# Layer 0 of a graph network: TensorE makes the counts of two steps in a row, then two steps' share of the sums

## The reference, cut to what matters

```python
h = relu(layernorm(x))                        # x: 6250 nodes x 128
def sage(h, Wl, bl, Wr):                      # 206250 edges (src, dst), sorted by dst
    msg = segment_sum(h[src], dst, 6250)
    cnt = segment_sum(ones, dst, 6250)
    return (msg / max(cnt, 1)) @ Wl.T + bl + h @ Wr.T
h = relu(batchnorm(sage(h, Wl0, bl0, Wr0)))   # layer 0: 128 -> 256
h = relu(batchnorm(sage(h, Wl1, bl1, Wr1)))   # layer 1: 256 -> 256
out = x + log_softmax(sage(h, Wl2, bl2, Wr2)) # layer 2: 256 -> 128
```

## Time and profile before

| | |
|---|---|
| median of 3 runs | 1443.36 us (1443.16 to 1446.37) |
| the profiled execution | 1447.48 us, of which the span of the core's instructions is 1445.6 us |
| layer 0 | up to about 556 us of the span |
| TensorE | busy 1347.1 us, 93% of the span |
| VectorE, ScalarE, GpSimd | busy 40%, 36% and 39% of the span |
| VectorE and ScalarE in layer 0 (60 to 545 us) | 369.66 and 385.70 of 485 us |
| granted TensorE clock | 0.997 of full speed in the mean |

### The profile page before, as it was taken

The page is one execution under the profiler, slowest core; times in us unless marked ns, Lnnn a source line. Parts: engine busy times, 40 slices in busy tenths (PEclk is TensorE's granted clock), DMA queues, the critical chain, the costliest instruction groups (busy, mean ns, idle before and its releaser), DMA issues.

```text
span 1445.6 us, 31363 instructions
## 1 busy us (share of the span) xinstructions
PE 1347.1 (93%) x13653; PEld 828.9 (57%) x13653; DVE 581.0 (40%) x1081; ACT 520.4 (36%) x848; POOL 562.7 (39%) x562
## 2 busy tenths in 40 slices
PE   1399999999998999999999999999999999899997
PEld 0277777777776778664444444444447754444445
DVE  6977767686869862221111111102102212222223
ACT  4897878778787783430000000000000520000001
POOL 3423140404132100005566666665661026566650
PEclk9999999999999999999999999999999999999999
DMA  6334554445454443446666666665652688898983
GB/s 165 99 140 165 199 197 179 169 140 209 187 205 175 144 157 99 172 137 234 203 223 218 230 226 217 227 228 181 226 180 75 199 297 297 290 322 314 327 304 99
DMA packets 91988, 291.14 MB, mean 201 GB/s; under 512 B 17539, under 2 KB 53013, under 8 KB 88613
## 3 DMA queue, kind: packets, MB, share of 16 engines
q1 hardware_dynamic: 63596, 228.73, 44.3%
q0 software_dynamic: 21824, 55.44, 12.6%
q10 hardware_dynamic: 6424, 4.88, 1.1%
HBM read 197.78 MB, written 91.22 MB: 200 GB/s over the span
## 4 chain that ended last, share of the span: by engine, by line
PE 78%; ACT 6%; DMA 5%; issue 4%; DVE 4%; POOL 3%; ACTq 0%; DVEq 0%; SPq 0%; POOLq 0%
PE bank L1603 27%; PE bank L1180 16%; PE cells L1603 12%; PE cells L1172 6%; DMA hots<-table,src_i 3%; PE bank L1856 3%; PE cells L1213 2%; POOL hots L514 2%; PE cells L1669 2%; ACT ring L650 2%; PE bank L1606 2%; ACT junk L598 2%; PE bank L1186 1%; PE bank L1188 1%; DMA parts<-in_pairs_dram,last_i 1%
## 5 line engine op out<-in xcount | busy, mean ns | idle before, releaser
L514 POOL DMA_INDIRECT hots<-table,src_i x444 | 420.5, 947 | 455.4 <-DMA table<-parts 216.8
L1603 PE MATMUL bank<-ring,parts 128*128 128x500 f16 x2058 | 463.0, 375 | 0.0
L650 ACT CAST ring<-cells 128x980 f16<-128x980 f32 (+1 forms) x325 | 337.6, 1056 | 103.0 <-PE cells L1172 96.5
L1603 PEld LDWEIGHTS bank<-ring,parts 128*128 128x128 f16 x2058 | 192.7, 96 | 226.0 <-issue 13.5
L1180 PE MATMUL bank<-ring,parts 128*128 128x250 f16 (+1 forms) x2450 | 317.8, 272 | 2.2 <-ACT ring L650 2.2
L875 DVE TENSOR_TENSOR hots<-iotas,tab 128x980 f16<-128x980 f16 (+3 forms) x262 | 245.5, 997 | 4.6 <-ACT tab L614 4.6
L1180 PEld LDWEIGHTS bank<-ring,parts 128*128 128x128 f16 (+1 forms) x2450 | 215.8, 98 | 33.8 <-ACT ring L650 3.0
L1603 PE MATMUL cells<-ring,parts 128*128 128x500 f16 (+1 forms) x980 | 215.9, 373 | 0.0
L721 ACT ACTIVATE agmg<-cells,isp 128x124 f32<-128x124 f32 x20 | 7.3, 364 | 472.9 <-PE cells L1222 472.9
L1603 PEld LDWEIGHTS cells<-ring,parts 128*128 128x128 f16 (+1 forms) x980 | 90.9, 96 | 112.7 <-issue 9.0
L1172 PE MATMUL cells<-hots 64*128 64x49 f16 x4670 | 105.6, 186 | 40.3 <-DVE hots L875 36.8
(11 more groups left out here) (211 smaller groups left out, 965.1 us busy)
## 6 DMA issues: line engine op xcount, KB each, us to landing
ring<-c_blocks SPq DMA_DIRECT2D x120, 750.0 KB, 6.1
c_blocks<-ring SPq DMA_DIRECT2D x25, 3062.5 KB, 10.7
ring<-c_blocks SPq DMA_DIRECT2D x40, 812.5 KB, 5.0
rcb<-rc_row SPq DMA_DIRECT2D x69, 125.0 KB, 8.7
hots<-table,src_i POOLq DMA_INDIRECT x444
Z<-in_x_dram SPq DMA_DIRECT2D x4, 768.0 KB, 6.4
table<-parts SPq DMA_DIRECT2D x2, 1536.0 KB
table<-parts ACTq DMA_DIRECT2D x2, 1536.0 KB
```

Of the source, the lines that this page charges most:

```text
L514: pool.indirect_dma_start(out=got[layer][:, 5 * (r % NGOT) + i, :], out_offset=None, in_=tables[layer], in_offset=bass.IndirectOffsetOnAxi ...
L650: act.copy(blk[c % 2][:, :, :].rearrange("p a (d g) -> p a d g", d=GD)[:, :, :, GPS * i:GPS * i + n], cells[t % 2][:, :, 0:n * NA].rearran ...
L1603: ins = pe.matmul(bank[b][:, 0:2 * BD].rearrange("p (s d) -> p s d", s=2), lhs, ring[0:r, :, BD * a:BD * a + BD], start=(a, part) == (0, 0 ...
```

## The change

```diff
@@ pe_layer0, in step i of round c, behind the counts
                     if c >= 1:
-                        if i == 0:
+                        if i == 1:
                             pe.wait_ge(a_cells, NST * c)
                             if c >= 3:
                                 pe.wait_ge(v_mean, c - 2)
-                        upto = len(work) * (i + 1) // NST
+
+                        upto = len(work) * (i + 1) // NST if i % 2 or i == NST - 1 else done
                         for a, part in work[done:upto]:
```

## The result

The changed kernel takes **1459.49 us** (median of 4 runs, 1457.58 to 1461.34) beside 1443.26 us of the kernel before (4 runs): a ratio of 1.0112, 95% interval 1.0093 to 1.0132. That is 16 us slower, where 1442 was forecast. The profiled execution took 1459.71 us, its span is 1457.9 us. Layer 0 ends, by the first matmul that follows it, at 570.1 us instead of 556.2; what comes after lasts as long as before (887.8 us against 889.4). So all of the loss, 13.9 us in these two executions, lies in layer 0 (they are 12.2 us apart; the medians are 16.2 apart).

What follows compares the result with a forecast made beforehand. Layer 0 was taken as bound by TensorE's list: 97 saved passage pairs at 0.21 give 20 us, nearly all given back in waits, chiefly for ScalarE's copies, leaving about 1 us: 1442 us, range 1433 to 1450.

Steps and rivals of the forecast that it cites:

- what a passage costs: TensorE's switch between counts and sums: 0.10 to 0.11 us; a joined pair takes 2.35 instead of 2.56, 0.21 less.
- The 0.80 before the counts of step 9: Steps 6 to 9: ScalarE's two L694 delay the copy of step 7, so these counts wait 0.80 us, in 18 rounds.
- the 0.08 of an ordinary pair: Joined pairs: odd counts come at 2.62 us, their buffer is free at 2.70, a wait of 0.08 for ScalarE's copy.
- the `pe_ends` rounds: Five rounds where L1158 comes 0.96 us earlier; the wait for VectorE covers the one of 0.80; gain 0.96.
- The turns' waits: Steps 10 and 11, rounds 4, 8, 12, 16, 20: waits of 0.9 or 0.4 us; loss 0.24, or 0.87 in 16 and 20.
- Steps 4 and 5: The product of 1.79 us lies between the groups, the number of passages stays, ScalarE catches up: gain 0.
- the five cycles: Gains and losses summed over cycles of four rounds: -0.02 to 0.4 up to round 13, about -0.2 each later; together +0.3.
- the samplings: Five times, over steps 11, 12, 0, 1: copies 1.90 us apart; gain of 0.11 to 0.18 kept.
- rival 3: VectorE sets the pace, covering waits for ScalarE: less than 3 us either way, 1440 to 1445; within the forecast's 0.7 chance.
- the wait in step 4 of rounds 8, 12, 16 and 20: TensorE arrives earlier than VectorE's one-hots and waits up to 0.7 us, giving back what it gained since `pe_ends`.
- Rival 1: ScalarE's copies keep up and step 9 does not wait: 18 x 0.80 come back, 1428 us; chance 0.1.
- Rival 2: TensorE and ScalarE in lockstep: copies free 0.06 us later cost 115 pairs 7 us, 1449; pair above 2.45; chance 0.2.

Runs made afterwards that it cites:

- after_spread2: The changed kernel with each block's store cut into seven pieces, issued at steps 0, 1, 2, 4, 5, 6 and 8 of the next round: 1444.1 us.
- before_spread2: The kernel before with its block store cut into seven pieces, issued at steps 0, 1, 2, 4, 5, 6 and 8 of the next round: 1445.4 us.
- before_long: The kernel before with each block stored twice, to two places, by one transfer of 6 MB: 1488.8 us, ratio 1.0295.

## Why the prediction was wrong

**Right: what a passage costs.** 2.35 us for a joined pair was forecast and 2.35 is in the trace. Steps 0 to 3 take 5.14 us before and 4.80 after in an ordinary round, a gain of 0.34, as forecast.

**Right: the waits for the copies.** The 0.80 before the counts of step 9 is 0.79; the 0.08 of an ordinary pair is the 0.1 inside the row of 0.80. About 25 us of waits were forecast. The view adds up to 19.1, in 31 pieces, and it shows 28 of them, those directly behind other counts, 0.17 too short: some 24. The wait before step 9 was forecast as 18 x 0.80 = 14.4; in after_spread2 it stands in sixteen rounds, and the delays add up to 11.9. As forecast, there is none in the `pe_ends` rounds; rounds 20 and 21 have none either.

**Right: ends and turns.** In round 3 the counts follow L1158 after 2.66 us, as forecast, and the wait shrinks to 0.64, from 1.40 in the same round before and in the earlier trace rows. The turns' waits rise from 1.2 to 3.1 us.

**So the sum holds where nothing else waits.** With the store cut and the issue waits gone the measured ratio to the kernel before is 1.0007 [0.9993, 1.0022], which takes in the forecast 0.9993. Beside its own control, before_spread2, the changed kernel is 1.35 us faster in the medians. There is some luck in how close this is. Steps 4 and 5 were put at 0 and cost 0.09 in nearly every round (4.26 us before, 4.35 after), nearly 2 us in all; the waits before step 9 were put 2.5 us too high. And the five cycles were summed as +0.3, while the terms as printed (with 0.11 for the samplings) give 0.38 - 0.02 - 0.02 - 0.23 - 0.23 = -0.1. All of this is inside the error that the prediction named. VectorE's pace, rival 3, moved no more than was allowed for it: TensorE's waits for it are 18.3 us before, 14.9 in the changed kernel and 17.5 in after_spread2, and the wait in step 4 of rounds 8, 12, 16 and 20, put at up to 0.7, shows as 0.32 at most.

**Wrong: the step that took TensorE's list for granted.** The part on what bounds the kernel says "layer 0 is bound by how fast TensorE gets through its list", and the sum was made of passages and of waits for other engines. That TensorE must also be given its instructions, 16 KB at a time, over the same DMA engines that carry 3 MB at the start of every round, has no term in it; the store itself was left out. The kernel before just manages (0.9 us in 24 rounds). The changed one runs steps 0 to 3 faster, beside the store, and runs dry: 12.9 us of issue waits, and about 1.4 us more for the half clock after the longest (0.77 + 0.32 + 0.35 for the three rows behind it). The 12.0 by which the issue waits grew and the 1.4 are 13.4 of the 13.9 us; taking the cause away gave back 15.4 us of the median. The row "issue 0.9" stood in the view that the earlier trace rows were taken from, and I left it out as small. It was the one sign in that view that this supply had little to spare.

A page had it the other way. The Trainium skill, Runtime: NRT & Kernel Launch, Instruction fetch mechanics, says that a sequencer fetches its program in blocks of 16 KiB while it runs the one before, and that crossing a block is "mostly hidden". The trace agrees on the size (111 packets, 1.82 MB) and, for the changed kernel, not on the cost: 12.9 us in layer 0.

**Rival 1 did not come true** in the changed kernel, since step 9 waits there. Its price was half right: if step 9 did not wait, 14 us were to come back, and with L694 at step 5 and no issue waits it was 7.0 us (1444.1 to 1437.0). Of the 11.9 us of delays before step 9 in after_spread2 the move takes away 9.3, and leaves the small ones of ordinary pairs and those of rounds 22 to 24; 1.3 us of it are lost again in step 11 of round 15, where a wait of 1.25 for VectorE follows. **Rival 2**, lockstep, gave the right side for the wrong reason: a pair takes 2.35 and not 2.45.

The range, 1433 to 1450, was made of errors of the terms that were there. A term that was missing is in no such range.

## What to carry to other kernels

Where an engine gets through thousands of short instructions, read the "issue" row of its waits and the DMA queue of kind "instruction" beside the large transfers: an engine that is made faster next to a transfer of megabytes may run out of program, and here one small issue wait before the change was the warning. A store that nobody awaits is then not free; two pieces with a gap of a few microseconds between them cured it here, two pieces without a gap did not, and seven pieces of which the last was issued too late cost more than the issue waits. To tell such a wait from others, look for the fetch whose end stands just ahead of it. And of two engines in turns, look for what stands between the paired copies: moving one small activation by a step was worth 7 us in the joined order and nothing in the old one.

## What the runs showed of the hardware

- A store of 3062.5 KB in one transfer holds the 16 DMA engines at 90.1% for 9 us. In round 11 no fetch of instructions was served in that time. Over the 24 rounds of the changed kernel the first fetch started 4.2 to 11.1 us after the store's issue, and with stores of 6125 KB (before_long) 5.5 to 12.9 us.
- TensorE, when it had run out of instructions, went on 1.2 to 1.6 us after the end of a fetch of 16 KB, in all twelve issue waits of the changed kernel's layer 0.
- After an idle stretch of 3.19 us TensorE's granted clock went to 0.50 (1.2 GHz) for 3.4 us; after the issue waits of 1.58 and 1.42 us in rounds 18 and 19 it stayed at 1.00.
- The wait in brackets behind a row of short matmuls is 0.17 us less than the delay from start to start (0.62 against 0.79), and waits of 0.1 to 0.2 us inside a merged row of forty show only in its length (0.80 and 0.91 against 0.70).
- Of four chips three agree for the same kernel (1443.5 to 1443.7 us), and one is 1.3% slower (1462.65 us).
